# A fused attention and mixture-of-experts kernel: second bias added in PSUM, single last tiles, a new order of calls

## What is computed

```python
raw = softmax(x @ w_gate); top_vals, top_idx = top_k(raw, 2); w = softmax(top_vals)
comb = zeros((t, E)).at[arange(t)[:, None], top_idx].add(w)
hmid = gelu(einsum('td,edi->tei', x, we1) + be1[None], approximate=False)
eout = einsum('tei,eid->ted', hmid, we2) + be2[None]
out = einsum('te,ted->td', comb, eout)
```

## Time and profile before

| | us |
|---|---|
| median of three runs | 1145.48 |
| the profiled execution's own time | 1147.27 |
| its span in the profile | 1145.5 |
| PE busy (7141 matmuls and transposes) | 1115.4 (97%) |
| DVE busy (2016) | 856.9 (75%) |
| ACT busy (1565) | 736.6 (64%) |
| POOL busy (509) | 636.7 (56%) |
| mean granted clock of PE | 0.993 |

### The profile page before, as it was taken

The page is one execution under the profiler, slowest core; times in us unless marked ns, Lnnn a source line. Parts: engine busy times, 40 slices in busy tenths (PEclk is TensorE's granted clock), DMA queues, the critical chain, the costliest instruction groups (busy, mean ns, idle before and its releaser), DMA issues.

```text
span 1145.5 us, 20473 instructions
## 1 busy us (share of the span) xinstructions
PE 1115.4 (97%) x7141; PEld 1014.4 (89%) x7141; DVE 856.9 (75%) x2016; ACT 736.6 (64%) x1565; POOL 636.7 (56%) x509
## 2 busy tenths in 40 slices
PE   8999999999999999999999999999999999889996
PEld 7998889999999999899999999999999998777995
DVE  6777767777777777777777777777777777867698
ACT  4667856666666666666666666666666665664753
POOL 2226656465656565655555555555555556846663
PEclk9999999999999999999999999999999999999998
DMA  5003312121212121212121212121212112221001
GB/s 171 1 1 79 107 38 52 38 60 38 51 39 60 38 51 38 60 38 51 37 61 38 51 37 61 37 52 42 56 37 52 42 38 47 67 91 38 1 20 56
DMA packets 46302, 56.55 MB, mean 49 GB/s; under 512 B 5940, under 2 KB 29176, under 8 KB 46200
## 3 DMA queue, kind: packets, MB, share of 16 engines
q1 hardware_dynamic: 45368, 54.19, 19.0%
q10 hardware_dynamic: 832, 1.05, 0.3%
HBM read 17.47 MB, written 4.19 MB: 19 GB/s over the span
## 4 chain that ended last, share of the span: by engine, by line
PE 84%; DVE 5%; POOL 4%; issue 4%; ACT 2%; DMA 1%; SPq 0%; POOLq 0%; DVEq 0%; ACTq 0%
PE ps_m L427 51%; PE ps_s L427 21%; PE ps_t L569 10%; POOL work L2081 1%; POOL work L2085 1%; DVE acc L1670 1%; POOL qk_lo L2092 1%; DVE acc L1609 1%; DVE rows L1502 1%; DVE acc L1680 1%; PE ps_m L480 1%; DMA acc<-in_L_attn_x 0%; DVE pT_lo L1576 0%; PE ps_m L627 0%; POOL hT_lo L2063 0%
## 5 line engine op out<-in xcount | busy, mean ns | idle before, releaser
L2081 POOL TENSOR_TENSOR work<-work,rope 128x512 f32<-128x512 f32 x128 | 166.4, 1300 | 228.4 <-DMA work<-work 228.4
L1576 DVE TENSOR_TENSOR pT_lo<-ps_t,pT_hi 128x512 fp32r<-128x512 f32 (+3 forms) x408 | 210.7, 550 | 38.6 <-ACT pT_hi L1077 36.4
L1077 ACT ACTIVATE pT_hi<-ps_t 128x512 fp32r<-128x512 f32 (+3 forms) x408 | 183.1, 489 | 72.0 <-PE ps_t L569 71.7
L1569 DVE CUSTOM_DVE_ANT_0 ps_s<-ps_s,causal 128x128 f32<-128x128 f32 (+7 forms) x272 | 203.3, 766 | 6.7 <-PE ps_s L427 4.2
L2092 POOL TENSOR_TENSOR qk_lo<-work,qk_hi 128x512 fp32r<-128x512 f32 x128 | 163.2, 1295 | 24.6 <-ACT qk_hi L1034 24.6
L2085 POOL TENSOR_TENSOR work<-work 128x512 f32<-128x512 f32 x128 | 167.5, 1309 | 10.0
L1609 DVE SCALAR_TENSOR_TENSOR acc<-ps_m,rinv,acc 128x256 f32<-128x256 f32 x272 | 118.5, 478 | 61.6 <-PE ps_m L427 61.4
L1028 ACT ACTIVATE work<-ps_m,bqk 128x512 f32<-128x512 f32 x128 | 88.8, 694 | 111.6 <-PE ps_m L427 111.6
L1070 ACT ACTIVATE prob_b<-ps_s,nmax 128x640 f32<-128x640 f32 (+3 forms) x136 | 130.6, 960 | 23.4 <-DVE nmax L1569 20.3
L427 PE MATMUL ps_s<-qk_hi 128*128 128x384 f32 (+5 forms) x384 | 141.0, 367 | 2.8 <-POOL qk_lo L2092 2.0
L427 PE MATMUL ps_m<-pT_hi,v_hi 128*128 128x512 f32 (+3 forms) x384 | 131.6, 343 | 3.5 <-DVE pT_lo L1576 2.4
(11 more groups left out here) (195 smaller groups left out, 2839.5 us busy)
## 6 DMA issues: line engine op xcount, KB each, us to landing
work<-work SPq DMA_DIRECT2D x256, 128.0 KB, 2.3
acc<-in_L_attn_x SPq DMA_DIRECT2D x8, 256.0 KB, 4.5
wst<-in_L_ffn_wq SPq DMA_DIRECT2D x16, 128.0 KB, 2.5
wst<-in_L_ffn_wk SPq DMA_DIRECT2D x16, 128.0 KB, 2.4
wo_st<-in_L_ffn_wo SPq DMA_DIRECT2D x16, 128.0 KB, 2.1
wst<-in_L_ffn_wv SPq DMA_DIRECT2D x8, 256.0 KB, 3.0
x_rows<-acc SPq DMA_DIRECT2D x4, 512.0 KB, 4.0
wst<-in_L_ffn_we SPq DMA_DIRECT2D x8, 256.0 KB, 2.9
```

The lines of the kernel that those rows point to most:

```text
L1077: act.activation(pT_hi[:, slots, cols], t_bank(u, i, j)[:, 0:size * P].rearrange("p (j q) -> p j q", q=P), ACT.Copy).then_inc(t_hi.sem, t_ ...
L1569: dve.tensor_tensor_reduce(s, s, causal[:, T - (i + 1) * P:T], -1.0, ABOVE_ALL, ALU.add, ALU.min, accum_out=nmax[:, u % 2, i:i + 1]).then_ ...
L1576: dve.tensor_tensor(pT_lo[:, slots, cols], t_bank(u, i, j)[:, 0:size * P].rearrange("p (j q) -> p j q", q=P), pT_hi[:, slots, cols].bitcas ...
L2081: pool.tensor_tensor(qs[:, x % 2, :], qs[:, x % 2, :], sin_t[:, c * CH:(c + 1) * CH], ALU.mult).then_inc(sin_done.sem, sin_done.up(u, x))
```

## The change

Bias: mix_bias is gone. For all experts but the last of the second half, mix adds be2 to the 128x512 result in its PSUM bank and then multiplies by comb and adds to acc. For the last one ACT multiplies be2 by comb (scale_bias), and POOL adds that to acc (add_scaled) before the four experts of that half are mixed. Tail: the last tile gets a PSUM bank of its own (of ps_t), the last two row tiles are mixed, normalized and stored singly. All calls in start() and ends() on all five queues have a new order; head(u) has not changed. In the code parts below twelve columns of indentation are taken off.

```diff
 END_JOB = 6
+LAST_EXPERT = (BATCH - 1, NC * EXPERTS - 1)
+TAIL = ((0, 1), (2,), (3,))
...
+
+scaled = prob_s[:, 0:T]
+last_tile = ps_t[:, 0, 0:D]
...
+            out = ps_s[:, n % 4, t * D:(t + 1) * D]
+            if (b, u) == LAST_EXPERT and (g, t) == (1, 1):
+                out = last_tile
             for i in range(2):
-                last = product(ps_s[:, n % 4, t * D:(t + 1) * D],
+                last = product(out,
                                (mid_part(0, u, i)[:, tile], mid_part(1, u, i)[:, tile]),
                                (we2_part(0, e, i), we2_part(1, e, i)), i == 0, i == 1)
+            if (b, u) == LAST_EXPERT and (g, t) == (1, 0):
+                last.then_inc(tile_mm, 1)
         last.then_inc(out_mm.sem, out_mm.up(b, n))

...
+def scale_bias():
+    b, e = LAST_EXPERT[0], EXPERTS - 1
+    act.wait_ge(be2_ld, 16)
+    act.wait_ge(gated.sem, gated.at(b))
+    for t in range(TC):
+        ins = act.activation(scaled[:, t * D:(t + 1) * D], be2[:, e, :], ACT.Identity, bias=zero[:, 0:1],
+                             scale=comb[:, b, TC + t, e:e + 1])
+    ins.then_inc(bias_scaled, 1)
...
 def tail_stats(g):
-
-    tiles = (2 * g, 2 * g + 1)
-    dve.wait_ge(mixed.sem, mixed.at(1, 14 + g))
+    tiles = TAIL[g]
+    if g == 1:
+        dve.wait_ge(tile_mixed, 1)
+    else:
+        dve.wait_ge(mixed.sem, mixed.at(1, 14 if g == 0 else 15))
...
     link(last, ln_links)
-    part = slice(2 * g, 2 * g + 2)
-    dve.tensor_scalar(var[:, 1, 0, part], mv[:, 1, part, 1], EPS, None, ALU.add).then_inc(tail_var, 1)
+    part = slice(tiles[0], tiles[-1] + 1)
+    dve.tensor_scalar(var[:, 1, 0, part], mv[:, 1, part, 1], EPS, None, ALU.add).then_inc(tail_var[g], 1)

 def tail_rows(g):
-    dve.wait_ge(tail_rstd, g + 1)
+    dve.wait_ge(tail_rstd[g], 1)
     dve.wait_ge(stored[1].sem, stored[1].at(0))
-    for t in (2 * g, 2 * g + 1):
+    for t in TAIL[g]:
         last = dve.tensor_scalar(out_st[:, TC + t, :], acc[:, 1, TC + t, :], mv[:, 1, t, 0:1],
                                  rstd[:, 1, 0, t:t + 1], ALU.subtract, ALU.mult)
-    last.then_inc(tail_rows_done, 1)
+    last.then_inc(tail_rows_done[g], 1)

 def ln_apply(job, c):
...
-def mix_bias(b, u):
-    c, e = u // EXPERTS, u % EXPERTS
-    if b == 0 and u == 0:
-        dve.wait_ge(be2_ld, 16)
+def mix_tile(t):
+    b, (c, e) = LAST_EXPERT[0], (NC - 1, EXPERTS - 1)
+    if t == 2:
+        dve.wait_ge(tile_mm, 1)
+        dve.wait_ge(mixed.sem, mixed.at(b, 13))
+        out = ps_s[:, 3, 0:D]
+    else:
+        dve.wait_ge(out_mm.sem, out_mm.at(b, 15))
+        out = last_tile
+    tile = TC * c + t
+    ins = dve.scalar_tensor_tensor(acc[:, b, tile, :], out,
+                                   comb[:, b, tile, e:e + 1], acc[:, b, tile, :], ALU.mult, ALU.add)
+    if t == 2:
+        ins.then_inc(tile_mixed, 1)
+    else:
+        ins.then_inc(mixed.sem, mixed.up(b, 15))
+
+def mix(b, u, g):
+    c, e, n = u // EXPERTS, u % EXPERTS, 2 * u + g
+    bank = ps_s[:, n % 4, :]
+    dve.wait_ge(out_mm.sem, out_mm.at(b, n))
+    if (b, u) != LAST_EXPERT:
+        if n == 0 and b == 0:
+            dve.wait_ge(be2_ld, 16)
+        halves = bank.rearrange("p (t d) -> p t d", d=D)
+        link(dve.tensor_tensor(halves, halves, be2[:, e:e + 1, :].to_broadcast([P, 2, D]), ALU.add), mix_links)
     if e == 0:
         dve.wait_ge(gated.sem, gated.at(b))
         dve.wait_ge(x1_added.sem, x1_added.at(b, c))
+        if c and b:
+            dve.wait_ge(bias_added, 1)
     else:
-        dve.wait_ge(mixed.sem, mixed.at(b, 2 * u - 1))
-    for t in range(TC):
-        tile = TC * c + t
-        last = dve.scalar_tensor_tensor(acc[:, b, tile, :], be2[:, e, :], comb[:, b, tile, e:e + 1],
-                                        acc[:, b, tile, :], ALU.mult, ALU.add)
-    last.then_inc(bias2.sem, bias2.up(b, u))
-
-def mix(b, u, g):
-    c, e, n = u // EXPERTS, u % EXPERTS, 2 * u + g
-    dve.wait_ge(bias2.sem, bias2.at(b, u))
-    dve.wait_ge(out_mm.sem, out_mm.at(b, n))
+        dve.wait_ge(mixed.sem, mixed.at(b, n - 2))
     for t in range(2):
         tile = TC * c + 2 * g + t
-        last = dve.scalar_tensor_tensor(acc[:, b, tile, :], ps_s[:, n % 4, t * D:(t + 1) * D],
+        last = dve.scalar_tensor_tensor(acc[:, b, tile, :], bank[:, t * D:(t + 1) * D],
                                         comb[:, b, tile, e:e + 1], acc[:, b, tile, :], ALU.mult, ALU.add)
     last.then_inc(mixed.sem, mixed.up(b, n))
...
-    pool.wait_ge(tail_var, g + 1)
-    if g == 0:
-        pool.wait_ge(rows_end.sem, rows_end.at(END_JOB, 1, TC - 1))
-    part = slice(2 * g, 2 * g + 2)
-    pool.tensor_tensor(rstd[:, 1, 0, part], var[:, 1, 0, part], minus_half[:, 0:2],
-                       ALU.pow).then_inc(tail_rstd, 1)
+    pool.wait_ge(tail_var[g], 1)
+    pool.wait_ge(rows_end.sem, rows_end.at(END_JOB, 1, TC - 1))
+    part = slice(TAIL[g][0], TAIL[g][-1] + 1)
+    pool.tensor_tensor(rstd[:, 1, 0, part], var[:, 1, 0, part], minus_half[:, 0:len(TAIL[g])],
+                       ALU.pow).then_inc(tail_rstd[g], 1)
...
+def add_scaled():
+    b, c = LAST_EXPERT[0], NC - 1
+    pool.wait_ge(bias_scaled, 1)
+    pool.wait_ge(x1_added.sem, x1_added.at(b, c))
+    x = flat(acc[:, b, tiles_of(c), :])
+    pool.tensor_tensor(x, x, scaled, ALU.add).then_inc(bias_added, 1)
...
         sp.dma_start(dram_rows(A["out"], b, c)[:, 2 * g:2 * g + 2, :],
                      out_st[:, TC * c + 2 * g:TC * c + 2 * g + 2, :]).then_inc(stored[c].sem, 16)
     stored[c].up(b)

+def store_tail(g):
+    b, c = LAST_EXPERT[0], NC - 1
+    first, end = TAIL[g][0], TAIL[g][-1] + 1
+    sp.wait_ge(tail_rows_done[g], 1)
+    sp.dma_start(dram_rows(A["out"], b, c)[:, first:end, :],
+                 out_st[:, TC * c + first:TC * c + end, :]).then_inc(tail_stored, 16)
+
 def finish():
-    for c in range(NC):
-        sp.wait_ge(stored[c].sem, stored[c].at(1))
+    sp.wait_ge(stored[0].sem, stored[0].at(1))
+    sp.wait_ge(stored[1].sem, stored[1].at(0))
+    sp.wait_ge(tail_stored, 16 * len(TAIL))

...
```

The order, where the prediction speaks of it. PE, first block, and then last units and experts:

```diff
     transposes(1, 2)
-    first_outputs(1, 0, 0)
     transposes(1, 3)
+    ln_transpose(2, 0)
     scores(1, 5)
-    ln_transpose(2, 0)
-    scores(1, 6)
     first_outputs(1, 0, 1)
     project_v(1, 3)
     project_q(2, 0)
     transposes(1, 4)
+    scores(1, 6)
     ln_transpose(2, 1)
     scores(1, 7)
     project_q(2, 1)
...
+    transposes(2, 2)
     scores(2, 4)
-    transposes(2, 2)
-    project_q(3, 1)
     transposes(2, 3)
     scores(2, 5)
+    project_q(3, 1)
+    outputs(2, 0)
+    transposes(2, 4)
+    ln_transpose(3, 0)
     scores(2, 6)
-    outputs(2, 0)
-    ln_transpose(3, 0)
-    transposes(2, 4)
...
-    out_project(LAST - 2, 1, 0)
-    transposes(LAST - 1, 1)
     scores(LAST - 1, 4)
     transposes(LAST - 1, 2)
+    out_project(LAST - 2, 1, 0)
+    out_project(LAST - 2, 1, 1)
+    transposes(LAST - 1, 3)
     scores(LAST - 1, 5)
-    transposes(LAST - 1, 3)
     project_q(LAST, 1)
-    out_project(LAST - 2, 1, 1)
     outputs(LAST - 1, 0)
+    transposes(LAST - 1, 4)
     scores(LAST - 1, 6)
     project_q(LAST, 2)
-    project_q(LAST, 3)
-    transposes(LAST - 1, 4)
     scores(LAST - 1, 7)
     transposes(LAST - 1, 5)
+    project_q(LAST, 3)
     out_project(LAST - 1, 0, 0)
+    transposes(LAST - 1, 6)
     scores(LAST, 0)
+    ln_transpose(4, 0)
     scores(LAST, 1)
+    transposes(LAST - 1, 7)
     scores(LAST, 2)
-    transposes(LAST - 1, 6)
-    ln_transpose(4, 0)
-    transposes(LAST - 1, 7)
     gate_logits(0, 0)
     out_project(LAST - 1, 0, 1)
     ln_transpose(4, 1)
     scores(LAST, 3)
     outputs(LAST - 1, 1)
     transposes(LAST, 0)
+    transposes(LAST, 1)
     gate_logits(0, 1)
-    transposes(LAST, 1)
-    scores(LAST, 4)
     transposes(LAST, 2)
-    scores(LAST, 5)
     out_project(LAST - 1, 1, 0)
     transposes(LAST, 3)
+    scores(LAST, 4)
+    scores(LAST, 5)
+    outputs(LAST, 0)
+    transposes(LAST, 4)
     out_project(LAST - 1, 1, 1)
     scores(LAST, 6)
-    outputs(LAST, 0)
-    transposes(LAST, 4)
+    transposes(LAST, 5)
+    scores(LAST, 7)
     out_project(LAST, 0, 0)
-    scores(LAST, 7)
-    transposes(LAST, 5)
+    transposes(LAST, 6)
     out_project(LAST, 0, 1)
-    transposes(LAST, 6)
     expert_in(0, 0)
     transposes(LAST, 7)
     expert_in(0, 1)
     outputs(LAST, 1)
     expert_out(0, 0)
+    ln_transpose(5, 0)
+    expert_out(0, 1)
     out_project(LAST, 1, 0)
     out_project(LAST, 1, 1)
-    ln_transpose(5, 0)
-    expert_out(0, 1)
     expert_in(0, 2)
     gate_logits(1, 0)
     expert_in(0, 3)
...
     expert_out(0, 2)
     ln_transpose(5, 1)
     expert_out(0, 3)
+    expert_out(0, 4)
+    expert_in(0, 5)
     gate_logits(1, 1)
-    expert_in(0, 5)
-    expert_out(0, 4)
     expert_in(0, 6)
+    expert_in(0, 7)
     expert_out(0, 5)
-    expert_in(0, 7)
     expert_out(0, 6)
     expert_in(1, 0)
+    expert_out(0, 7)
     expert_in(1, 1)
-    expert_out(0, 7)
+    expert_out(1, 0)
     expert_in(1, 2)
-    expert_out(1, 0)
```

(122 more changed lines are left out.)

471 lines of the change are left out of this document (233 added, 238 removed).

## The result

The changed kernel takes 1124.45 us (median of 4 runs, 1124.2 to 1125.3) against 1145.26 for the kernel before beside it; the ratio is 0.9819, 95% interval 0.9802 to 0.9835. The forecast was 1134.3, the gain 20.8 us where 11.2 was forecast, and the time lies outside the range. The profiled span is 1122.8 us, 22.7 shorter. That is 1.9 more than the medians say, because the profiled execution of the kernel before took longer than most of its runs (1147.27, 1.8 above the median), and that of the changed kernel did not (1124.56).

What follows compares the result with a forecast made beforehand. PE was taken as the bound, idle 30.1 of 1145.5 us. Gains of 2.6 (experts and tail), 1.9 (first block) and 6.7 (last units) sum to 11.2, so 1134.3 us; own range 1129.5 to 1138.5, widened to 1142.5.

Steps and rivals of the forecast that it cites:

- the last units: PE's stretch from 940 to 1041.7 us: the new order shortens waits and clock loss, 6.7 us gained after a deduction.
- Idle time left, 4.3: Last units: PE waits still found under the new order sum to 4.3 us, for 9.7 before.
- the walk: Going through the new order of calls, with the old trace's durations, to find which waits stay.
- Deduction of 2.2 for one unseen hold: Last units: 2.2 us off the 8.9 gain for one held DVE instruction that mean durations can't show.
- Busy time, 3.5 counted: Last units: the loss from the lower PE clock falls from 4.5 to 1.0 us.
- First block, 1.9: Up to 152 us: three PE waits shortened or covered, 2.7 us, less a possible new wait: 1.9 us gained.
- Experts and tail, 2.6: After 1041.7 us: 0.45 at expert_out(1, 7), 1.7 behind the last matmul, 0.5 from two smaller waits: 2.6 us.
- A: Rival: the order moves waits without shortening them, only 2.6 + 1.9 us stay: 1141.0 us (1138.5 to 1143.2); chance 0.22.
- B: Rival: a drain after added DVE instructions costs 1.2 us in the last chain: 1135.5 us; chance 0.05.
- C: Rival: slower, the clock stays at half from 990 to 1036 us: 1151.5 us; chance 0.04.
- D: Rival: no change, new waits also eat the first block's and tail's 4.5 us: 1145.5 us (1143.2 to 1147.8); chance 0.06.
- E: Rival: the hand count is right without the deduction and more waits go than found: under 1129.5 us; chance 0.06.

Runs made afterwards that it cites:

- e11: Changed kernel with the old order of calls in the last units, the new one from outputs(LAST, 1) on: 1135.54 us, ratio to the kernel before 0.9920.
- e16: Kernel before with the changed kernel's order of SP transfers in the last units, other engines as before: 1148.94 us, ratio 1.0020.
- e4: Kernel before with three matmul groups done twice, same results, placed next to idle times of the last units: 1145.35 against 1146.12 us, ratio 0.9991.
- e7: Changed kernel with the last expert's bias added in PSUM too, without the ACT scaling and POOL addition: 1127.1 us.
- e6: Changed kernel with its last four tiles finished in two pairs, instead of one pair and two single tiles: 1124.61 us.
- e3: Kernel before with the changed kernel's order of calls, old SBUF bias passes ahead of each expert's mixes, tail in pairs: 1142.81 us, ratio 0.9973.
- e5: As e3, but bias passes behind each expert's two mixes, except the last expert of each half: 1135.94 us, ratio 0.9904 to the kernel before.
- e10: Changed kernel with the old order of calls from outputs(LAST, 1) on: 1134.89 us, ratio 0.9906 to the kernel before.
- e2: Kernel before with the new bias operations and single last tiles, all in the old order of calls: 1145.91 us, ratio 0.9992.
- e15: Changed kernel with the transfers of the last units and experts in SP's old order: 1130.0 us.
- e13: As e10, with POOL's two 128x1024 additions moved behind three 128x512 low parts: 1132.84 us.

## Why the prediction was wrong in size

The direction and the places were right; all three terms were too small, one of them by 8 us. The step that failed is the last units, "Gain 8.9. From this I take off 2.2 [...] 6.7 us"; measured, 14.9 between the two profiles, and 11.1 by the medians of e11 and the changed kernel. The bullets go by the profiles, since the forecast's terms came from one.

- **Idle time left, 4.3; measured 1.9.** Of the four waits the walk kept, the one before outputs(LAST, 1) was 0.19 instead of 1.0, the ones around transposes(LAST, 6) 0.3 instead of 1.4, that at transposes(LAST, 2) was not there; 0.60 stood where 1.0 was said, and one of 0.81 (982.53) was missed. ln_apply(4, 1) did not lose "most of its 3.3 us hold": it took 3.35 us, against 1.37 for the first four rows. POOL did wait for ACT, as the walk had it, but only until 0.6 us after ln_apply(4, 1) had started:

```profile
985.21 3.35 DVE L1528 TENSOR_SCALAR rows<-acc,mv,rstd 128x256 f32<-128x256 f32 x4
...
985.80 2.61 POOL L2089 TENSOR_TENSOR hT_lo<-hf,hT_hi 128x512 fp32r<-128x512 f32 x2 [1.61 <-ACT hT_hi L999]
```

  It only holds nothing up any more: PE has no wait of over 0.05 us while it runs. A walk on mean durations whose ready times lie within half a microsecond of each other cannot tell such waits from none, and I took each as there.
- **Deduction of 2.2 for one unseen hold: 0.** Holds of that size are real (3.46 us for 1.37 in e16), but no second one cost PE time in the changed kernel.
- **Busy time, 3.5 counted (clock loss 4.5 to 1.0); measured 7.0.** The clock's 4.5 fits e4's profile, but all of it went. The other 2.5, the price of stopping and restarting beyond the idle time itself, had no term.
- Together 2.4 + 2.2 + 3.5 = 8.1 of the 8.2 us missed.
- **The base.** That "median and span coincide" was chance: the span is that of a longer execution, the median the whole time of a usual one. The changed kernel's span (1122.8) is 1.8 below its own time too. The terms were sized on a profile 1.8 us slower than the median, so a sum that was right for the profile would have promised about 1.8 us too much gain for the medians.

**First block, 1.9; measured 3.7 to 4.0.** The three waits of the earlier trace rows went as the walk had it (0.20 is left of the second), two more that it did not count went too (0.54 us at 99.81, 0.15 at 138.84), and the 0.8 taken off for a new wait was not needed. The start stays, as forecast: a wait of 1.26 us at 8.48 us is gone, but only other matmuls fill it, so that the idle time up to the loop fell by 4.8 us (8.6 to 3.8; forecast, to 6.7) and the time by less.

**Experts and tail, 2.6; measured 3.8.** The wait before the last expert_out was forecast at 0.5 and is 0.53. Behind the last matmul 8.3 was forecast and 7.2 measured. DVE had less left to do when the last matmul ended (tile 2's mix ended at 1115.49, 0.1 before it; the walk had it 0.25 behind), and each single tile's statistics took 0.80 us, not 0.95. Of the tail's 2.8 us the last bias off DVE's chain bought 1.6 (e7) and the single tiles 0.1 (e6); the rest was not tried by itself.

**Bias in PSUM.** 0.691 us per addition (taken: 0.69), 0.73 to the start of the next (0.69 + 0.04), 20.7 us in all: as forecast. That "between 1041.7 and 1125 this buys nothing" was right for the old order and wrong for the new: with the old passes the experts took 14.9 us (e3) and 5.8 us (e5) longer than in the changed kernel. That the parts add up was the hidden premise of the sum. By the ratios the new order of the experts is worth 0.0087 or 10.0 us behind the new units (e10 to changed), and the operations 0.0085 or 9.7 us under the new order (e5 to changed) and 0.9 in the old one (e2, an interval that holds zero).

**The transfers.** "The rotations' loads are not behind load_expert(2, 3)" stood in the walk without a price. It is worth 5.5 us in the changed kernel (e15) and costs 2.3 in the old one (e16).

**Rivals.** A (the order only moves waits) falls. B (a drain behind each added instruction, which the Trainium skill, "VectorE: DVE Perf Modes", section "The DRAIN you can't avoid", would put at 0.42 us, as an estimate) falls. The trace does not agree with that rule: the dependent instruction started 0.04 us after the end of the addition, and the one after the pair of 0.88 us started 0.79 us after the pair did. C and D fall. E, under 1129.5, is what happened, at a chance of 0.06: half of its condition, my walk without the deduction, was in my hands and would have given 1132.1; without the 0.8 taken off in the first block too, 1131.3. Both are still above 1129.5.

## What to carry to other kernels

Where several in-order queues feed the bounding engine, an order is worth what the queues make of it together: parts of this change gave 0.4% (first block), 0.1% (operations), 0.3 to 1.0% (the whole order on the old operations), 0.7% (first block and last units) and -0.2% (transfers), and the whole 1.8%. So a part tried alone says little, and a sum over parts is a guess. Count a wait at its idle time plus the lower clock and the restart behind it, between these two profiles almost twice the idle time (14.9 us for 7.8). And look where the profiled execution lies among the runs before its stages are taken as the kernel's. When a transfer or an engine becomes earlier, look at what its instructions will then run beside.

## What was not expected of the hardware

A DVE tensor_tensor on small SBUF operands took as long as the POOL instruction beside it: 0.19 us free, 1.2 to 1.3 beside 128x512, 2.1 to 2.4 beside 128x1024 (e10, e13); a reciprocal of 128x8 between them took 0.20 all the same. The additions with one operand in PSUM were 0.682 to 0.700 us in all 30 instances, whatever POOL did. And with 2.7 us of useless matmuls in it, the kernel before took no longer (0.9991, an interval that holds 1); in the profile its last units were shorter, 98.2 us against 100.8, with the clock at 1.00 (e4).
